# Attention stage of a fused block on one core: the twelve steps of neighbouring head groups overlapped by one step, and the score matmuls for the row maxima placed by a written table

## The reference

```
x: (2, 1024, 512);  xn = layernorm(x)
s = attention(xn):  q, k, v = clip(xn @ Wqkv.T, +-8);  q = layernorm(q), k = layernorm(k) over all 512 columns
    32 heads of 16;  scores = q.k / 4 + slope[head] * (key - query), causal;  s = softmax(scores) @ v @ Wout.T
g = silu(ffn(xn)):  dequantized 4-bit gate/up/down weights, silu(gate) * up, down
out = x + s * g
```

## Time and profile before

| | |
|---|---|
| median of three runs | 1124.32 us (1123.53 to 1124.39) |
| the profiled execution | 1123.91 us, of which 1121.8 us are the span of the trace |
| first scores of group 0, last group | 191.2 us, 685.79 us |
| second stage | 191 to 713 us |
| TensorE clock granted, mean | 0.993; 0.91 in 191 to 226 us, 1.00 in the rest of the second stage |

### The profile page before, as it was taken

One profiled execution on the slowest core, in us unless ns is written; L12 is line 12 of the kernel. 1 busy time (PEld: TensorE's weight loads), 2 busy tenths in 40 slices (PEclk: granted clock), 3 DMA queues, 4 the chain that ended last, 5 costly groups with the idle time before them and its releaser, 6 DMA issues. The chain is left out here.

```text
span 1121.8 us, 18965 instructions
## 1 busy us (share of the span) xinstructions
PE 1043.7 (93%) x6242; PEld 635.6 (57%) x6242; DVE 926.4 (83%) x2147; ACT 725.7 (65%) x1167; POOL 465.1 (41%) x554
## 2 busy tenths in 40 slices
PE   5999987999999999999999999899999999999995
PEld 4788764333333433333333333487778778777874
DVE  6788897787878888788888875579989998998896
ACT  3666565676667667666666667567747766774774
POOL 2666645111111111111111111039946864994786
PEclk9999998999999999999999999999999999999998
DMA  6254753453543334454343433100120011012001
GB/s 212 77 155 142 214 144 94 133 119 72 142 108 95 113 100 119 75 142 109 89 120 96 120 77 105 39 1 0 39 70 7 1 55 59 1 39 75 1 1 38
DMA packets 98584, 95.32 MB, mean 85 GB/s; under 512 B 28030, under 2 KB 80950, under 8 KB 98486
## 3 DMA queue, kind: packets, MB, share of 16 engines
q1 hardware_dynamic: 96854, 93.72, 29.9%
q10 hardware_dynamic: 1632, 0.39, 0.2%
HBM read 72.45 MB, written 21.23 MB: 84 GB/s over the span
## 5 line engine op out<-in xcount | busy, mean ns | idle before, releaser
L883 ACT ACTIVATE pr<-pair 128x1024 f32<-128x1024 f32 (+3 forms) x384 | 293.1, 811 | 151.2 <-PE pair L999 97.0
L266 DVE CUSTOM_DVE_ANT_0 bank<-bank,sg 128x384 f32<-128x384 f32 (+1 forms) x488 | 227.5, 521 | 65.6 <-PE bank L276 62.1
L1527 PE MATMUL pair<-xc_lo,w_gu 128*128 128x512 f32 x448 | 181.5, 405 | 4.5 <-DVE xc_lo L1363 4.5
L1528 PE MATMUL pair<-xc_hi,w_gu 128*128 128x512 f32 x448 | 175.3, 391 | 0.0
L269 DVE TENSOR_REDUCE mx<-bank 128x1 f32<-128x512 f32 x240 | 150.1, 682 | 8.9 <-PE bank L276 8.2
L1375 DVE SCALAR_TENSOR_TENSOR gate<-pair,sgu,gate 128x512 f32<-128x512 f32 x168 | 124.5, 741 | 25.7 <-PE pair L1528 24.1
L1166 POOL TENSOR_TENSOR yt<-yt,tmp 128x512 f32<-128x512 f32 x96 | 124.2, 1314 | 0.0
L276 PE MATMUL bank<-ks,qs 108*128 108x512 bf16 (+3 forms) x384 | 107.7, 329 | 5.3 <-DVE mx L266 5.1
L1527 PEld LDWEIGHTS pair<-xc_lo,w_gu 128*128 128x128 f32 x448 | 84.1, 188 | 37.3 <-DVE up L1375 6.6
L1156 POOL TENSOR_TENSOR h_lo<-gate,h_hi 128x512 fp32r<-128x512 f32 x56 | 72.5, 1296 | 76.6 <-ACT h_hi L1209 76.6
L994 PE MATMUL pair<-s_sb,xin_c 111*128 111x512 bf16 (+3 forms) x384 | 95.1, 332 | 7.7 <-ACT dt L395 2.9
(11 more groups left out here) (125 smaller groups left out, 2121.4 us busy)
## 6 DMA issues: line engine op xcount, KB each, us to landing
stk<-parts SPq DMA_DIRECT2D x16, 768.0 KB, 5.7
zst<-in_z_all SPq DMA_DIRECT2D x24, 448.0 KB, 4.0
sst<-in_w_all SPq DMA_DIRECT2D x24, 448.0 KB, 4.7
xin_c<-in_x SPq DMA_DIRECT2D x32, 256.0 KB, 3.3
s_sb<-stk SPq DMA_DIRECT2D x96, 64.0 KB
xin_c<-stk SPq DMA_DIRECT2D x96, 64.0 KB
qs<-stk SPq DMA_DIRECT2D x96, 64.0 KB
ks<-stk SPq DMA_DIRECT2D x96, 64.0 KB
```

The lines of the kernel that those rows point to most:

```text
L266: dve.tensor_tensor_reduce(out=src, in0=src, in1=tri[:, 512 - w:512], scale=1.0, scalar=-3.0e38, op0=ALU.add, op1=ALU.max, accum_out=dst). ...
L883: act.activation(pr[e % 3][:, 2 * p:2 * p + 2, 0:w], pair[p][:, :, 0:w], ACT.Exp, scale=SCALE)\
L1527: pe.matmul(GB[j % 4], w, xc_lo[:, k, :], start=True, stop=False)
L1528: pe.matmul(GB[j % 4], w, xc_hi[:, k, :], start=False, stop=True).then_inc(gu_done, 1)
```

## The change

The order on PE and DVE in the second stage now comes from a table `PLAN` of 36 rows, one for each place. A digit is the query tile, `u` marks upper keys. Eight pieces of query tiles 2 and 3 in the first steps are the group's own; the digits 0, 1 and all of 4 to 7 are for the next group. Five upper pieces of the next group stand in the first step, where none stood before.

- The last `pv` of a group is issued in step 0 of the next group, and O0 in the second place of step 3 of the next group. `copy_o` of the lower block follows the exponentials of the next group's step 0.
- D1 is an ordinary entry of the ring of three banks, in the second place of step 10, with O1 behind it. DVE copies it and ACT sends it ahead of the exponentials of step 11. D0 moves from step 5 to step 4 and is sent at step 6, O1 from step 9 to step 10.
- SP asks for the part `b=1` when the scores of step 7 stand in `pair[1]`, for the part `b=0` (without the values) when those of step 11 do, and for the values after the last `pv`.
- `job 1` and its conversion move from the end of the even group to the odd group, the conversion ahead of the exponentials of step 2.

```diff
-        LATER_KEYS = len(EARLY) // 2
-        (spread, and the places that it gives)
...
+        PLAN = (
+            "4u 7u", "5u", "6u 6u",
...
+            "5u 6u", "7u 4u", "D0 4 4u",
...
+            "7 7", "5", "5",
+            "1", "0", "0",
+            "0", "D1 O1", "1",
+            "0 1", "", "1",
+        )
...
-                        sp.wait_ge(pv_done, PV0 + NSTEP * i + FIRST)
+                        sp.wait_ge(s_full[1], full(i, FIRST - 1, 1))
                         load(sp, i + 2, s, 1)
+                        sp.wait_ge(s_full[1], full(i, NSTEP - 1, 1))
+                        load(sp, i + 2, s, 0, values=False)
                         sp.wait_ge(pv_done, PV0 + NSTEP * i + NSTEP)
-                        load(sp, i + 2, s, 0)
+                        load_v(sp, i + 2, s)
...
+                        if e == place_of["D0"] + 2:
+                            act.wait_ge(m_free, number(i, "D0") + 1)
+                            send_d(act, s, 0, d0_in)
+                        if e == place_of["D1"] + 1 and not last:
+                            act.wait_ge(m_free, number(i, "D1") + 1)
+                            send_d(act, 1 - s, 1, d1_in)
+                        if e == JOB1_AT and s == 1:
+                            convert(ip, 1)
...
+                        exps(i, e, 0)
+                        exps(i, e, 1)
+                        if e == 0 and i > 0:
+                            copy_o(i - 1, 1)
...
-                            send_d1(act, 1 - s, full_d1(i), i + 2, pair[0][:, 0, :])
-                    copy_o(i, 1)
-                    if s == 0:
-                        convert(ip, 1)
...
+                        if x == of_kind["upper"][0]:
+                            pe.wait_ge(stk_in[1 - s][1], LOADS[1] * (i // 2 + 1 + s))
...
                     for e in range(NSTEP):
...
-                        slot0_free(i, e, last)
                         second(i, s, e, 0)
+                        for part in range(3):
+                            if part == 1:
                                 second(i, s, e, 1)
+                            if part == 2 and e > 0:
                                 pv(i, s, e - 1)
+                            elif part == 2 and i > 0:
+                                pv(i - 1, 1 - s, NSTEP - 1)
+                            for x in plan[3 * e + part]:
+                                if present(x, i):
+                                    fill(i, s, x)
...
-                    pv(i, s, NSTEP - 1)
-                    ring(i, s, tail[BEFORE:], last)
```

More of the change, by code:

```diff
@@ L20 @@
+from collections import Counter
 from contextlib import ExitStack
@@ L232, in build @@
-        parts_of_plan = (spread(LATE[HEAD:], 0, OWN_END), spread(EARLY[:LATER_KEYS], OWN_END - 1, LOW_AT),
-                         spread(EARLY[LATER_KEYS:], LOW_AT, EARLY_END), spread(LATE[:HEAD - TAIL], EARLY_END, PLACES))
-        plan = {h: sum((part[h] for part in parts_of_plan), []) for h in range(PLACES)}
-        plan[3 * D0_AT + 2].append("D0")
-        plan[3 * O1_AT + 2].append("O1")
-        tail = LATE[HEAD - TAIL:HEAD] + ["O0"]
-        own = [x for h in range(PLACES) for x in plan[h] if x in LATE[HEAD:] or isinstance(x, str)] + ["O0"]
@@ L240, in build @@
-        order = [x for h in range(PLACES) for x in plan[h]] + tail
-        RING = len(order)
-        assert RING % 3 == 0
+        OWN = LATE[HEAD:]
         HEAD_ORDER = LATE[:HEAD // 2] + EARLY + LATE[HEAD // 2:HEAD]
         PREP = len(HEAD_ORDER)
-        number = ({x: n for n, x in enumerate(order)}, {x: n for n, x in enumerate(own)})
-        def at(x, last):
-            return number[last is True][x]
-        def ring_bank(x, last):
-            return b_m[(PREP + at(x, last)) % 3]
-        def base(i):
-            return PREP + RING * i
+        PLACES = 3 * NSTEP
@@ new lines, in build @@
+        plan = [[item(token) for token in row.split()] for row in PLAN]
+        in_order = [x for row in plan for x in row]
+        assert sorted(x for x in in_order if not isinstance(x, str)) == sorted(EARLY + LATE)
+        place_of = {x: h // 3 for h, row in enumerate(plan) for x in row}
+        of_kind = {name: [x for x in in_order if x in lot] for name, lot in
+                   (("own", OWN), ("early", EARLY), ("head", LATE[:HEAD]),
+                    ("upper", [x for x in EARLY if x[2]]), ("lower", [x for x in EARLY + LATE[:HEAD] if not x[2]]))}
@@ new lines, in build, with present, number @@
+        JOB_AT, JOB1_AT = 6, 2
+        def present(x, i):
+            if x == "O0":
+                return i > 0
+            if x in ("D0", "O1") or x in OWN:
+                return True
+            return i < NG - 1
+        ring_of = [[x for x in in_order if present(x, i)] for i in range(NG)]
+        ring_of[NG - 1].append("last O0")
+        place_in = [{x: n for n, x in enumerate(r)} for r in ring_of]
+        first_in = [PREP + sum(len(r) for r in ring_of[:i]) for i in range(NG)]
+        def number(i, x):
+            return first_in[i] + place_in[i][x]
@@ L860, in body @@
                 def body(i, s, ip, last):
-                    pool.wait_ge(m_free, base(i) + at(LATE[-1], last) + 1)
-                    pool.wait_ge(s_full[0], USES[0] * i + 1)
+                    if s == 1:
+                        job(ip, 1)
+                    pool.wait_ge(m_free, number(i, of_kind["own"][-1]) + 1)
+                    if i == 0:
+                        pool.wait_ge(s_full[0], 1)
+                    else:
+                        pool.wait_ge(m_full, number(i - 1, "D1") + 1)
                     chain(pool, mx0[:, :, :], 2 * i + 1)
```

163 lines of the change are left out of this document (71 added, 92 removed).

## The result

The changed kernel takes 1130.81 us (median of 11 runs, 1127.24 to 1143.24) against 1124.08 before (11 runs, 1123.22 to 1128.68): a ratio of 1.007, 95% interval 1.0054 to 1.0085. It is slower by 0.7%, where 1105 us, a gain of 1.7%, was forecast. The profiled execution took 1134.63 us, 3.8 above the median.

What follows compares the result with a forecast made beforehand. PE, busy 94% in mid second stage, was taken as near its bound, with only its gaps to win. Savings of 14 x 1.3 + 2.2 - 1.0 = 19.4 us from 1123.91 us gave a forecast of 1105 us, range 1087 to 1121.

Steps and rivals of the forecast that it cites:

- Step 3: From D1 to the next group: D1's transfer lands 3.6 us after issue (2.7 to 4.55), next group begins at 31.3 us.
- step 4: Upper keys for a group's start: load starts at 21.3 us, lands 2.76 after its last issue, allowing a start at 31.05.
- step 6: Lower keys asked for earlier, first used in the next group's fifth step: costed at nothing, as were values and D0.
- step 2: D1 on PE: issued 27.1 us into the group (26.8 to 27.7) instead of 28.6.
- signs of being wrong: Groups at 30.3 us without PE waits, D1 issued later than 27.7, or first scores waiting over 2 us for keys.
- step 1: PE's work unchanged, its waits removed: 2.8 us in all, so a group without waits takes about 30.0 us.
- rival D: Key load right behind the weights: keys land 3.8 us later, at 35.3; groups take 34.9, kernel 1152 us; chance 0.11.
- Step 5: Weight conversion moved into odd groups: delays exponentials at most 0.3 us, costed at nothing in full groups.
- Step 7: End of second stage: group 14 takes about 30.3 us, 2.2 less; group 15 takes 1.0 us more.
- rival B: Everything arrives in time: groups run at PE's own 30.0 to 30.3 us, kernel 1086 us; chance 0.16.

Runs made afterwards that it cites:

- keys_ahead: Changed kernel with the upper-key load issued ahead of the weight job instead of behind it; 1085.6 us, ratio 0.9661.
- before_early: Kernel before the change, with only its upper-key load asked for as early as in the changed kernel, behind the weight job; 1123.71 us, ratio 0.9992.
- own_first: Changed kernel with the group's own eight pieces in its first two steps and the next group's upper keys only after them; 1115.3 us, ratio 0.9922.
- lower_late: Changed kernel with the lower-half load asked for where it was before, after the group's last product with the values; 1113.97 us, ratio 0.9892.
- light: Changed kernel with each weight job after the first fetching 128 of its 896 columns, leaving out the rest of the weights; 1095.69 us, ratio 0.9741.
- keys_step8: keys_ahead with the upper-key load asked for one half step later; 1112.86 us, ratio 0.9897.
- warm: Changed kernel with dummy 512-column matmuls on PE: ten ahead of the wait for D1, eight behind a group's first scores; 1135.51 us, ratio 1.0095.
- before_ahead: Kernel before the change, with its upper-key load issued earlier, ahead of the weight job, and the old order kept; 1174.58 us, ratio 1.0421.

## Why the prediction was wrong

The gain in PE's own pace was there. What failed are the two landings (steps 3 and 4), each priced by rows with other neighbours, the lower keys put at nothing (step 6), and a clock that was not in the sum. Together they made groups 1 to 13 33.8 us long instead of 31.4.

**What held.** In group 5 D1 comes onto PE 388.70 - 362.06 = 26.6 us into the group (step 2 said 27.1, ends 26.8 and 27.7, so it lies just under the lower one), and ACT issues it 0.53 us later (0.57 said). That is a group at the full clock; over groups 1 to 13 ACT issues D1 27.2 to 32.3 us in, and two of the prediction's own signs of being wrong are met: D1 later than 27.7, and over 2 us of waiting for keys (2.82 in group 2). The waits named in step 1 are gone, and PE's own pace, put at 30.0, is 29.4 in group 14, which waits for nothing. Group 14 was forecast at 30.3. The weight job, not step 7, starts the key load in group 5: 383.16 - 362.06 = 21.1 us (step 4 said 21.3). One average in the prediction is a little off: groups 1 to 14 before took (685.79 - 226.22) / 14 = 32.83 us, not 32.75, which is worth 1.1 us of the sum. And in rival D the landing that decides is 11.9 us after the first issue, not 11.5, since the keys are needed 0.45 us into the group.

**Step 3, the landing of D1.** I took 3.6 us, ends 2.7 and 4.55. For the kernel before, the 3.6 was exact: by the DMA completions in its trace 2.7 to 4.5 us in groups 1 to 13, 3.6 on average. The 3.73 of group 5, which the prediction later takes for a landing, was only a bound: D1 had landed there after 2.7. In the changed kernel it was 2.9 to 5.3 us, 4.3 on average; the 5.21 at the start of group 5 (356.85 to 362.06) lies above my upper end:

```profile
356.85 0.76 ACTq L402 DMA_DIRECT2D qs<-dt  x1
```

I drew the range from a kernel in which weights and key load lay apart. Issued 6.5 us behind the weights (8.2 before) and into the key load, with the DMA share at 0.98 in group 1, the small transfer took longer; in keys_ahead, issued ahead of the weights, it took 2.2 to 2.9. D1 is also the larger part of PE's waits, 18.7 of 30.8 us.

**Step 4, the landing of the keys.** I took 2.76 us behind the last issue, from the one place in the first stage where PE had waited for it. It was 5.9 us at group 2's start, and 2.9 to 5.8 in all, 4.9 on average. Nothing large is queued in front of the load of rows 9, nor right in front of the second stage's loads before the change, which landed 3.0 us after their last issue on average; so it was the wrong row to price this one by. The weights' own landing showed the crowding from their side (L812 and L819, median 4.7 us before, 5.9 after).

Mean landings over groups 1 to 13, in us after D1's issue and after the load's last issue, with the mean length of a group and PE's waits for both transfers from 258 to 640 us:

| run | D1 | keys | group | waits |
|---|---|---|---|---|
| before | 3.6 | 3.0 | 32.8 | 0.7 |
| before_early | 2.8 | 4.1 | 32.8 | 0 |
| changed | 4.3 | 4.9 | 33.8 | 30.8 |
| own_first | 4.1 | 4.7 | 32.2 | 15.6 |
| lower_late | 4.0 | 4.0 | 32.5 | 19.6 |
| light | 2.9 | 3.1 | 30.7 | 11.0 |
| keys_step8 | 3.4 | 3.1 | 31.9 | 18.5 |
| keys_ahead | 2.6 | 3.0 | 30.1 | 1.2 |

Rival D named the true cause, the weights right in front of the key load, and `light` shows it with a price of 35 us. Its account was half of it: it moved the keys alone and left D1 at 3.6. What I held against it, that a load with issues 0.47 us apart catches up, is true in part: the keys' slip was 3.1 us at group 2's start and 2.1 on average, not 3.8, and groups 1 to 13 took 33.8 us rather than 34.9. The kernel came out at 1131 and not at D's 1152.

**The clock, a term that was not in the sum at all.** Before, the stretch of rows 1 has the clock at 1.00; now it has 0.95. A mean of 0.95 over 389 us is some 39 us at 1.2 GHz (0.05 x 389 / 0.5), each such stretch behind a boundary at which PE had stood. In them PE gets through 19.5 us of work, so 19.5 us are lost by this estimate where PE sets the pace, less where it would have waited anyway. I had the waits of rival D at their own length; in ten of fourteen groups the waits at the start, 1.8 to 4.1 us together, brought a second loss behind them, in the steps ahead of D1. There it delays D1, the next boundary, and so the next wait. In group 2, which begins with the fall shown above, D1 is issued at +32.2 instead of about +27. The split between waits and clock is an estimate: groups 1 to 13 take 33.8 us on average, those of keys_ahead 30.1. Of the 3.7 us between them, the waits for the two transfers are 2.6 (29.6 us more in the 382 from 258 to 640, or 11.3 groups), which leaves about 1.1 for the clock. By the 1.5 us of own_first it would be some 1.5: seven groups have a mean of 0.95 and three one of 0.90 to 0.91, which I count twice, 13 x 1.5 = 20 us over 13 groups. Part of that falls into time in which PE would have waited anyway. No run took the clock's part away alone in the changed kernel, as `warm` paid for it in PE time.

**Step 6, lower keys for nothing.** lower_late gives 17 us of the changed kernel's time back. The load's first use was late enough; what I left out is, as I read it, what its bytes do to transfers in flight.

**Step 5 held** (no row of PE's waits names ACT), and before_ahead suggests that its worth was more than nothing: it lets the weights come late.

**Step 7.** Group 14 gave what was said and more, 29.4. Group 15 and the third stage together are 2.4 us longer than before against 1.0 said, with the clock at 0.98 there instead of 0.99. The first scores of the second stage come 1.7 us later; in the traces of all thirteen runs, whose first stage is the same, they come at 190.6 to 193.7 us, so this need not be the change. I tried nothing on either.

**The two rules that I weighed.** Both are from the Trainium skill (DMA: Bandwidth & Descriptors). The fixed cost of about 2.0 us (Anatomy of one DMA), which that section gives for transfers issued by GpSimd, lies near the 2.2 to 2.9 us of D1 in keys_ahead, issued by ACT, where no weights were ahead, and the kernel then gave the 1086 us of rival B; in the changed kernel it did not fit, with 2.9 to 5.3. The Trainium skill's ordering rule (same page, Queues, rings and completion order) pointed at the danger. I cited it, priced it at 11% and did not let it move the landing terms; the traces fit it as far as an issue 0.43 us ahead of the weights made 2.6 us and one 0.44 us behind their first 5.9. Order of issue is not all: in keys_ahead D1, issued 0.47 us behind the last key transfer, was used 0.57 us before the keys. Why a later increment waits, no run here shows.

## What to carry to other kernels

A transfer's landing time is not a property of the transfer alone but also of what was queued in front of it, on whichever queue (2.2 to 5.9 us here for the same 12 KB): when an edit moves an issue, price its landing by a row with the same neighbours, and ask of each big prefetch whether it can be issued behind the small, urgent ones. Freeing an engine from its waits also takes away the slack that made late transfers harmless, so the second wait must be costed at its worst row, not at its best. And at the full clock, a stop of PE of 1 to 3 us can cost more than itself: add a slow stretch behind it to the price, 1.5 us here, in the groups that had one.

## What the runs showed of the hardware

- A 12 KB transfer from ACT's queue landed in 2.6 us when it was issued 0.43 us ahead of a 0.92 MB pair on SP's queue, and in 5.9 us when issued 0.44 us behind the first of the pair. Issued into a load of fourteen transfers, 1.2 to 2.9 us ahead of its last issue and with no weights issued in the 17 us before, it landed in 3.1 to 3.8 us (keys_step8).
- The DMA share is time, not bytes: 0.98 in a window that moved 149 GB/s, 0.70 in one that moved 231.
- With those two transfers cut to a seventh, in the same places, the kernel was 35 us faster, and the DMA share from 226 to 640 us fell from 0.49 to 0.33.
- PE busy 92% of a stretch (291 to 680 us), with stops of 1 to 3 us at one place every 34 us, ran with stretches at 1.2 GHz (0.95 on average); with those stops filled by dummy matmuls the granted clock was 1.00. Not every stop brought one: behind the 2.53 us at the start of group 5 the clock stayed at its full level, while behind a single one of 1.73 us in own_first (group 4) it fell, with 0.70 on average from 320.3 to 326.0 us.
- One such stretch delayed what PE did 29 us into a group by 1.5 us (own_first, nine groups at 1.00 against five at 0.95).
